# Accumulator addresses worked out ahead of the pick, the one-hots and the weighing in a four-stage graph network on one NeuronCore

## The reference

```python
x = _layernorm(x + _L0_gnn_ref(x, edge_index, ...))   # edge MLP, mean over incoming edges
x = _layernorm(x + _L1_gnn_ref(edge_index, x))        # deg_inv_sqrt[row] * deg_inv_sqrt[col] * x[row], summed by col
x = _layernorm(x + _L2_gnn_ref(x, src, dst, ...))     # h[src] summed by dst, @ weight, relu
x = _layernorm(x + _L3_gnn_ref(x, edge_index, ...))   # 3 layers of GATv2 attention, 8 heads, batch norm between
```

## Time and profile before

| | |
|---|---|
| median of 3 runs | 5772.28 us (5757.51 to 5776.34) |
| the profiled execution's own time | 5782.98 us |
| its span, first to last instruction | 5781.3 us |
| mean granted TensorE clock | 0.942 |
| TensorE busy, matrix products | 5011.9 us (87%) |
| VectorE busy | 3668.6 us (63%) |
| ScalarE busy | 2137.7 us (37%) |
| GpSimd busy | 3814.9 us (66%) |

### The profile page before, as it was taken

One profiled execution on the slowest core, in us unless ns is written; L12 is line 12 of the kernel. 1 busy time (PEld: TensorE's weight loads), 2 busy tenths in 40 slices (PEclk: granted clock), 3 DMA queues, 4 the chain that ended last, 5 costly groups with the idle time before them and its releaser, 6 DMA issues.

```text
span 5781.3 us, 138144 instructions
## 1 busy us (share of the span) xinstructions
PE 5011.9 (87%) x47293; PEld 3469.3 (60%) x47293; DVE 3668.6 (63%) x7003; ACT 2137.7 (37%) x3988; POOL 3814.9 (66%) x3980
## 2 busy tenths in 40 slices
PE   5999999788887888599999985999999769999997
PEld 4777777688877888355555552555555535555554
DVE  6566554788777777456665674656666745656666
ACT  3222222455555666233333323333333233333331
POOL 4777776476646777577777726777777167777770
PEclk8999998899999999799999997999999989999998
DMA  4655555233323333344444423444444234444442
GB/s 115 175 167 169 166 168 149 74 94 85 83 71 95 105 100 98 68 123 124 122 125 129 123 78 76 125 125 125 124 122 126 66 90 124 126 124 122 123 122 63
DMA packets 689969, 663.38 MB, mean 115 GB/s; under 512 B 398324, under 2 KB 480699, under 8 KB 689275
## 3 DMA queue, kind: packets, MB, share of 16 engines
q1 hardware_dynamic: 557482, 489.13, 28.1%
q0 software_dynamic: 127424, 164.72, 14.8%
q10 hardware_dynamic: 4368, 0.70, 0.1%
HBM read 564.89 MB, written 89.17 MB: 113 GB/s over the span
## 4 chain that ended last, share of the span: by engine, by line
PE 56%; POOL 17%; issue 16%; DVE 6%; DVEq 1%; DMA 1%; ACT 1%; ACTq 1%; POOLq 0%
PE ps L1076 18%; PE ps L921 13%; POOL rows L368 12%; PE ps L1015 8%; POOL rows L381 6%; PE ps L1036 4%; PE ps L1050 3%; PE ps L936 3%; PE ps L1026 2%; PE ps L1001 2%; PE ps L995 1%; DVE region L1800 1%; DMA rows<-table,idx 1%; ACTq L759 1%; DVE acc L1825 1%
## 5 line engine op out<-in xcount | busy, mean ns | idle before, releaser
L381 POOL DMA_INDIRECT rows<-table,idx x2340 | 2249.6, 961 | 1091.0 <-issue 713.8
L1076 PE MATMUL ps<-region,hot 128*128 128x272 f32 x4992 | 1312.8, 407 | 175.2 <-DVE region L1778 85.6
L669 ACT ACTIVATE region<-ps 128x512 f32<-128x512 f32 x1248 | 677.6, 596 | 1679.4 <-PE ps L1015 1679.4
L1076 PEld LDWEIGHTS ps<-region,hot 128*128 128x128 f32 x4992 | 914.2, 193 | 470.1 <-issue 296.5
L1825 DVE TENSOR_TENSOR acc<-acc,ps 128x272 f32 x1248 | 544.2, 436 | 872.4 <-PE ps L1076 767.3
L921 PE MATMUL ps<-hot,region 128*128 128x192 bf16 (+1 forms) x9216 | 905.3, 258 | 51.0 <-DVE region L1652 28.5
L368 POOL DMA_INDIRECT rows<-table,idx x728 | 702.7, 965 | 258.9 <-issue 221.3
L921 PEld LDWEIGHTS ps<-hot,region 128*128 128x128 bf16 x9216 | 833.2, 103 | 63.3 <-DVE region L1652 31.7
L1800 DVE TENSOR_TENSOR region<-ps,region 128x1056 f32<-128x1056 f32 x582 | 724.1, 1250 | 48.2 <-issue 41.3
L1015 PE MATMUL ps<-xT,wcat 64*128 64x512 f32 x2496 | 712.2, 647 | 8.9 <-ACT region L669 8.9
L401 POOL DMA_INDIRECT rows<-table,idx x448 | 427.3, 954 | 197.5 <-issue 124.3
(11 more groups left out here) (306 smaller groups left out, 6798.3 us busy)
## 6 DMA issues: line engine op xcount, KB each, us to landing
hot<-hot_dram SPq DMA_DIRECT2D x624, 256.0 KB
turned<-turned_dram SPq DMA_DIRECT2D x624, 128.0 KB
rows<-table,idx POOLq DMA_INDIRECT x3516
hot_dram<-hot SPq DMA_DIRECT2D x104, 512.0 KB
region<-hot_dram SPq DMA_DIRECT2D x96, 512.0 KB
xwin<-table SPq DMA_DIRECT2D x1664, 24.0 KB
region<-r_dram SPq DMA_DIRECT2D x109, 256.0 KB, 5.9
region<-d_dram SPq DMA_DIRECT2D x104, 256.0 KB
```

The costliest lines, as they stand in the source:

```text
L381: pool.indirect_dma_start(rows[:, n % 2, j, :], None, table, bass.IndirectOffsetOnAxis(ap=idx[:, s:s + 1], axis=0)).then_inc(rows_in3[n % ...
L669: act.activation(rz[g % 2][:, 2 * t + side, :], ps[:, Z + side, :], ACT.Relu).then_inc(rz_made, 1)
L1076: mm = pe.matmul(ps[:, sum_bank(k, side, i), 0:PC + H], hot[:, b, 4 * side + 2 * i + j, :], px[b][:, 4 * side + 2 * i + j, :], start=(j == ...
```

## The change

In all four stages the register operations of a group's four addresses are moved ahead of the adds, into one block behind the load: `lower_ap` puts each address into a register there. In the edge pass the block stands before the pick; in a convolution before the pick of a dense group's first item, and before the one-hots for the next plain group; in attention right behind the load, before the weighing. The adds then take a ready register.

```diff
-            def add0(g):
+            def places0(g):
                 code = v.value_load(packed[0:1, g:g + 1], min_val=0, max_val=(1 << 20) - 1)
-                windows = [window_of(v, code, k) for k in range(4)]
+                places = [acc[:, bass.ds(window_of(v, code, k), 1), 0:HID + 1] for k in range(4)]
+                for place in places:
+                    v.lower_ap(place)
+                return [place.rearrange("p a c -> p (a c)") for place in places]
+
+            def add0(g, places):
                 v.wait_ge(agg_summed, g + 1)
-                for k, w in enumerate(windows):
-                    at = acc[:, bass.ds(w, 1), 0:HID + 1].rearrange("p a c -> p (a c)")
+                for k, at in enumerate(places):
...
                     turned0(s + 1)
+                places = places0(s - 2) if s >= 2 else None
                 if s + 2 < G:
                     pick0(s + 2)
                 if s >= 2:
-                    add0(s - 2)
+                    add0(s - 2, places)
...
-                def found(g):
+                def found(g, cols):
+
                     code = v.value_load(packed[0:1, g:g + 1], min_val=0, max_val=(1 << 20) - 1)
-                    return [window_of(v, code, k) for k in range(4)]
-
-                def add(w, cols, of, made, count):
-                    at = acc[:, bass.ds(w, 1), 0:cols].rearrange("p a c -> p (a c)")
+                    places = [acc[:, bass.ds(window_of(v, code, k), 1), 0:cols] for k in range(4)]
+                    for place in places:
+                        v.lower_ap(place)
+                    return [place.rearrange("p a c -> p (a c)") for place in places]
+
+                def add(at, of, made, count):
...
                         if kind == "dense":
                             stationary(dbase + i // 4 + 1, i % 4)
+                            if i % 4 == 0:
+                                places[i // 4 % 2] = found(DENSE[i // 4], C)
                             pick(i)
                             if i > 0:
                                 add_dense(i - 1)
                         else:
+                            to_add = found(PLAIN[i], 3 * C)
                             plain_one_hot(i + 1)
-                            add_plain(i)
+                            add_plain(i, to_add)
...
                 def found(k):
+
                     code = v.value_load(packed2[0:1, k:k + 1], min_val=0, max_val=(1 << 20) - 1)
-                    return [window_of(v, code, i) for i in range(4)]
+                    windows = [window_of(v, code, i) for i in range(4)]
+                    places = [acc[:, bass.ds(w, 1), 0:PC + H] for w in windows]
+                    for place in places:
+                        v.lower_ap(place)
+                    return windows, [place.rearrange("p a c -> p (a c)") for place in places]
...
-                def add_one(k, side, i, windows):
+                def add_one(k, side, i, places):
...
-                    at = acc[:, bass.ds(windows[2 * side + i], 1), 0:PC + H].rearrange("p a c -> p (a c)")
+                    at = places[2 * side + i]
```

More of the change, by code:

```diff
@@ L1665, in pick @@
                         "p j g c -> p j c g"), AX.X, ALU.add).then_inc(found_made, 1)
-                windows = {}
+                places = [None, None]
                 def add_dense(i):
-                    if i % 4 == 0:
-                        windows["dense"] = found(DENSE[i // 4])
                     v.wait_ge(dense_summed, 4 * dbase + i + 1)
-                    add(windows["dense"][i % 4], C, ps[:, DB[i % 2], 0:C], dense_added, 4 * dbase + i + 1)
+                    add(places[i // 4 % 2][i % 4], ps[:, DB[i % 2], 0:C], dense_added, 4 * dbase + i + 1)
                 def plain_one_hot(p_):
@@ L1680, in plain_one_hot, with add_plain @@
                                     ALU.is_equal).then_inc(plain_hot, 1)
-                def add_plain(p_):
+                def add_plain(p_, to_add):
                     at = base + p_
-                    ws = found(PLAIN[p_])
                     v.wait_ge(plain_summed, at + 1)
-                    for k, w in enumerate(ws):
-                        add(w, 3 * C, ps[:, at % 2, k * 3 * C:(k + 1) * 3 * C], plain_added, 4 * at + k + 1)
+                    for k, to in enumerate(to_add):
+                        add(to, ps[:, at % 2, k * 3 * C:(k + 1) * 3 * C], plain_added, 4 * at + k + 1)
                 def degree_groups(g):
@@ L1825, in add_one, with add @@
                     v.tensor_tensor(at, at, ps[:, sum_bank(k, side, i), 0:PC + H], ALU.add).then_inc(att_added, 1)
-                def add(k, side, windows):
+                def add(k, side, places):
                     for i in range(2):
-                        add_one(k, side, i, windows)
+                        add_one(k, side, i, places)
                 def scan_ahead(c, first):
@@ L1880, in attention @@
                         ts(fscale[:, :], ps[:, MISC, 0:H], first_hot[:, c:c + 1], 1.0, ALU.mult, ALU.add)
-                    windows = found(k) if 0 <= k < G else None
+                    windows, places = found(k) if 0 <= k < G else (None, None)
                     if phase == 2 and ends and c > 0:
@@ L1899, in attention @@
                         if windows:
-                            add(k, 0, windows)
+                            add(k, 0, places)
                         pick()
@@ L1905, in attention @@
                         if windows:
-                            add(k, 1, windows)
+                            add(k, 1, places)
                     elif phase == 1 and ends:
                         if windows:
-                            add(k, 0, windows)
+                            add(k, 0, places)
                         pick()
```

## The result

The changed kernel takes **5832.33 us** (median of 4 runs, 5816.3 to 5850.98) against 5774.31 us (4 runs, 5757.51 to 5782.05): ratio **1.011**, 95% interval 1.0088 to 1.0132. The prediction was 5830 us, slower, for delayed picks in the convolutions (+57), faster plain adds (-10) and open blocks in attention (+13).

A forecast was written before the change was run, and what follows sets the result against it. Bounds: gathers (edge pass, nearly convolution 2), TensorE-VectorE exchange (convolution 1), gathers and TensorE (attention). Terms -1 + 36 + 21 - 10 + 13 - 1 = +58 us on 5782.98 give 5841, as a median 5830; 8-in-10 range 5755 to 5915.

The forecast's parts named there:

- The block: A group's register operations in one place, load to engine instruction: 1.15 + 3F us, taken as 1.51 (1.33 to 1.90).
- F: Length of one fused register instruction in the block: taken as 0.12 us, bounds 0.06 and 0.25.
- rivals 2: No change: the fourth operation is as cheap as the others, faster adds pay the heads' delays; +14, 5786 us, chance 0.20.
- 3 (0.25): Much slower: the division in the fused instructions is dear, 0.25 us or more; 5929 us, chance 0.10.
- Rival 1: Faster: the sequencer works past waiting instructions, so blocks hide in waits for TensorE; -90, 5682 us, chance 0.15 with weaker forms.
- Edge pass: Block moved ahead of the pick costs zero, as gathers bound the pass; about -1 us from four adds at the end.
- Dense heads: First items of dense groups: the block delays the pick and TensorE waits; +36 us in convolution 2, +21 in convolution 1.
- Plain groups: Convolutions: one-hots 0.69 us late, three adds save 0.78, net -0.09 us at some 110 TensorE stalls: -10 us.
- Attention: Three places without slack per chunk of eight groups: +0.36 us, 36 times, +13 us (bounds -1 and +43).
- (b): Attention, step after a chunk's last: block before the first add makes it 0.69 us later, against 0.76 gained: -0.07.
- (c): Attention, another step later: open block behind L1282, 1.08 us becomes 1.77, less 0.26 at the second add: +0.43.
- the term of the ends: Last two adds of each attention layer and of each convolution: -1 us in all.

The follow-up runs named there:

- heads_behind: The changed kernel with the register block of a dense group moved behind its first pick and reduction: 5775.84 us, ratio 1.0014 to the kernel before.
- one_ahead: The changed kernel with the attention block moved ahead of the settling scans only, the step of the spread scale left open: 5828.39 us, ratio 1.0095.
- att_ahead: The changed kernel with the attention block moved ahead of both the settling scans and the wait for the spread scale: 5733.11 us, ratio 0.9950.
- before_ahead: The kernel before, its attention load and window operations moved ahead of settling scans and spread scale's wait, no addresses worked out ahead: 5754.29 us, ratio 0.9970.
- all_moved: The changed kernel with dense block behind pick and reduction, plain block behind next one-hots, attention block ahead of scans and scale's wait: 5631.51 us, ratio 0.9770.
- all_moved_tail: As all_moved, with the block of a layer's last eight groups also behind their first half weighing: 5621.72 us, ratio 0.9745 to the kernel before.

## Why the prediction was right, point by point

- **The block.** Predicted 1.15 + 3F = 1.51 us with F = 0.12. Measured 1.41 us from the load to the pick's start (1310.39 to 1311.80 in the trace); the fused instructions with a division take 92 to 106 ns (median of the four 94, the last one without it 65). So F was 0.10, at neither bound, and rivals 2 (F = 0.06) and 3 (0.25) fall.
- **Where the block starts.** In the timeline above the load of the plain block begins at 1306.29, 0.11 us behind the start of L1672, which had waited for L1665. In attention 216 of the 312 loads start 0.01 us (median) behind the start of the add L1838 ahead of them, an add for which VectorE had stood idle for 0.48 us (median). The prediction's wording missed one thing: the sequencer does go past an instruction that only waits its turn on the engine. The add L1644 between L1672 and the load starts at 1307.05, 0.76 us behind the load, and in a layer's last groups 21 loads start 0.4 us before the add ahead of them, which had no idle time before it. Rival 1 falls, and with it here the rule of the Trainium skill ("Perfetto Trace Analysis", section "DVE / Act Engine Instruction"), by which the sequencer is free once L1672 is pushed, while L1665 still runs (from 1305.52 on): the measurement decides.
- **Edge pass.** Predicted -1, measured -12 (-3 to -20). The pass is bound by gathers as said; the step that failed is the end, which was priced by the last four adds alone. Twelve adds, of three groups, come behind the last gather, and the clock there differs, for a reason that stays open.
- **Dense heads.** Predicted +57, measured +55, and the wait before the sums in convolution 2 is 82.4 us where over 80 was named. The size is right and its composition was not: I had +36 and +21 of waits. By stage it is 31 us in convolution 2 and 15 in convolution 1, in convolution 2 some 60% waits and 40% busy time. The step that failed is that a delay was priced by its wait alone.
- **Plain groups.** Predicted -10: the heads_behind kernel has 24 us less than before in convolution 1 and 7 more in convolution 2, -17; from the ratios, +8 for that kernel less attention's +33 and the edge pass's -12 leaves -13. The working said one-hots +0.69 late (0.56 in the timeline) against 0.78 saved; net -0.09 becomes -0.22. The waits of convolution 1 are hardly shorter, though (60.4 + 25.2 against 60.2 + 28.5): TensorE's busy time is, 552.0 against 575.2 us. So the size was met, but not by the shorter stalls that the working priced.
- **Attention.** Predicted +13, measured +33 (+24 to +43), inside the bound of +43 (with F = 0.25 the steps add up to 1.14 us, so +41). Single steps were met: (b) 0.60 us for 0.69 (idle time 1.29 instead of 0.69, medians of 36), (c) 1.68 us from L1282 to L1898 for 1.77. What failed is the term of the ends, a part of -1: behind a layer's last gather 129 to 131 us pass instead of 126 to 127, some +10 in three layers, where TensorE now waits 15.4 us in 17 places for the half weighings (5.1 in 4 before). The other part is the clock: over the gather stretches of the three layers TensorE's busy time rose by 20 us, from 2752 to 2772, which no term had. Those stretches grew by 15 us in all, so that TensorE's waits in them did not grow on balance, although +13 of waits was the whole term: the pick's wait grew by 10.4 us (85.6 to 96.0), and others shrank.
- **The sum.** +58 predicted, the three parts measured +58 together, the whole 64 by its ratio (58 between the medians). That the total fits so well is partly luck: the sum went by waits alone, and left out that TensorE's own work can take longer or shorter. Against the prediction the edge pass came out 11 us lower, the convolutions 10 us lower (+37 for +47) and attention 20 us higher, and these errors cancel.

## What to carry to other kernels

Before moving work ahead of a critical instruction, list for each possible place what the engine waits for there: the same register block cost 55 us more in front of a pick than behind the reduction that follows it, and 95 us more behind a wait of 4.2 us than ahead of it. Work out addresses early, but put the block under a long instruction or ahead of a long wait, and look whether the wait is really long (1.5 us in 39 places hides nothing). An engine's longest line of idle time under "issue" (159 us before a weighing) can be free, while 53 us in 36 places cost nearly twice their length.

## What was not expected of the hardware

In these runs a wait of TensorE costs more than its length where the granted clock falls with it. Around the 36 steps of the scale, in the 10 us that begin with L1898 (L1885 before), the mean granted clock over the profiled execution was 0.93 before, 0.88 in the change, 0.84 in `one_ahead` and 1.00 in `att_ahead`; the longest wait for the pick was 3.0, 3.3, 3.3 and 1.6 us. In four comparisons a third to a half of the difference was busy time (12.2 of 30.8, 26.6 of 55.3, 14.9 of 43.1, 16.5 of 31.5 us).

But clock and waits don't always go together. In `before_ahead` the longest wait for the pick was 2.1 us instead of 3.0, and yet the clock in those 10 us was 0.89 instead of 0.93 and the three layers' busy time 24 us more. In convolution 1 the change waits 17 us longer before L936 than the kernel before and is busy for 20 us less. And one kernel's value is in part chance: the four other kernels with the change's attention show 0.87, 0.88, 0.92 and 0.92 in those 10 us, the two others with the old one 0.94. The 1.00 of `att_ahead` stands in `all_moved` and `all_moved_tail` too. Whether it is the single long wait or the sum of them that lets the clock fall, these runs don't tell.

A fused register operation in which a division stands takes 90 to 106 ns over the whole program of the change, the block's last one, without a division, 65 (57 in the kernel before). Between the end of one and the start of the next pass 0.03 us.
